# Second graph layer's row gathers: up to four underway in the loop instead of three

## What is computed

```
h = (x @ W.T).reshape(n, 8, 64)
src, dst = edge_index
e = leaky_relu(einsum(h[src], a_src) + einsum(h[dst], a_dst), 0.2)
e = e * (1 + et_emb[edge_type]) * edge_weight[:, None]
e = exp(e - max over the edges of each dst)
alpha = e / (sum over the edges of each dst + 1e-10)
out[dst] += h[src] * alpha            # the messages
out = layernorm(out + x) * gamma + beta
```

## Time and profile before

| what | value |
|---|---|
| median of three runs | 1776.36 us |
| the profiled execution, own time | 1784.84 us |
| span of the profiled execution | 1783.1 us |
| PE busy in the span | 1662.2 us, 93% |
| DVE, ACT, POOL busy | 883.9, 500.9, 652.3 us |
| first and last gather of the layer start at | 1080.67 and 1259.09 us |

### The profile page before, as it was taken

One profiled execution on the slowest core, in us unless ns is written; L12 is line 12 of the kernel. 1 busy time (PEld: TensorE's weight loads), 2 busy tenths in 40 slices (PEclk: granted clock), 3 DMA queues, 4 the chain that ended last, 5 costly groups with the idle time before them and its releaser, 6 DMA issues.

```text
span 1783.1 us, 23533 instructions
## 1 busy us (share of the span) xinstructions
PE 1662.2 (93%) x7303; PEld 940.2 (53%) x7304; DVE 883.9 (50%) x2161; ACT 500.9 (28%) x1586; POOL 652.3 (37%) x756
## 2 busy tenths in 40 slices
PE   6989999999899999999999998797899999999998
PEld 4534444446655546455556766432444555555655
DVE  8878888888834443443443157785623101111322
ACT  1134444447422414133231225110200111111234
POOL 5868787873232323324342613666200000000000
PEclk9999999999999999999998997899899999999999
DMA  8031101005423123232216734356326121310020
GB/s 315 1 104 25 60 25 60 25 8 132 141 58 128 54 90 83 58 110 55 74 49 153 276 96 146 111 162 174 100 72 217 50 91 53 100 59 24 5 68 18
DMA packets 119614, 161.76 MB, mean 91 GB/s; under 512 B 49497, under 2 KB 61721, under 8 KB 119154
## 3 DMA queue, kind: packets, MB, share of 16 engines
q1 hardware_dynamic: 93056, 115.43, 21.0%
q0 software_dynamic: 18592, 29.91, 6.3%
q10 hardware_dynamic: 7890, 15.44, 2.7%
HBM read 145.26 MB, written 15.47 MB: 90 GB/s over the span
## 4 chain that ended last, share of the span: by engine, by line
PE 81%; DVE 9%; DMA 5%; issue 2%; ACT 2%; POOL 1%; ACTq 0%; DVEq 0%; POOLq 0%; SPq 0%
PE psum L373 79%; DMA ring<-tab_h,sd_t 2%; DMA arena<-tab_h,sd_t 1%; DVE stats L470 1%; DVE ring L1299 1%; DVE xn L2067 0%; PE psum L1028 0%; DVE xn L2073 0%; POOL ring L630 0%; DVE xn L2086 0%; ACT xT L414 0%; PE psum L2302 0%; DMA x<-in_x 0%; DVE ring L666 0%; DMA tab_h<-arena 0%
## 5 line engine op out<-in xcount | busy, mean ns | idle before, releaser
L373 PE MATMUL psum<-arena 128*128 128x384 f32 (+9 forms) x1804 | 315.3, 331 | 21.1 <-DVE arena L2688 8.0
L373 PE MATMUL psum<-arena,ring 128*128 (+1 forms) x1504 | 326.0, 363 | 9.5 <-issue 6.2
L373 PE MATMUL psum<-xT,ring 128*128 128x384 f32 x928 | 310.7, 495 | 6.8 <-ACT xT L414 4.2
L373 PE MATMUL psum<-ring,arena 128*128 128x512 f32 (+1 forms) x570 | 262.8, 604 | 15.3 <-DVE ring L666 10.5
L373 PEld LDWEIGHTS psum<-arena 128*128 128x128 f32 (+5 forms) x1804 | 195.1, 154 | 148.8 <-issue 74.7
L373 PE MATMUL psum<-ring,xT 128*128 128x512 f32 x552 | 251.1, 608 | 1.1 <-issue 0.7
L373 PEld LDWEIGHTS psum<-xT,ring 128*128 128x128 f32 x928 | 178.2, 193 | 133.2 <-issue 17.6
L373 PEld LDWEIGHTS psum<-arena,ring 128*128 128x128 bf16 (+1 forms) x1504 | 139.4, 115 | 131.3 <-issue 29.9
L373 PEld LDWEIGHTS psum<-ring,arena 128*128 128x128 f32 (+1 forms) x570 | 99.2, 187 | 140.4 <-issue 139.3
L1079 ACT ACTIVATE ring<-ring 128x128 f32<-128x128 f32 x416 | 123.3, 297 | 173.4 <-DVE ring L1365 161.4
L373 PEld LDWEIGHTS psum<-ring,xT 128*128 128x128 f32 x552 | 104.8, 195 | 124.1 <-issue 121.7
(11 more groups left out here) (478 smaller groups left out, 1737.0 us busy)
## 6 DMA issues: line engine op xcount, KB each, us to landing
ring<-in_L_ffn_w SPq DMA_DIRECT2D x22, 1024.0 KB, 7.3
ring<-in_L_gnn_m_w SPq DMA_DIRECT2D x8, 1024.0 KB, 6.1
ring<-in_L_ffn_expert_weights SPq DMA_DIRECT2D x8, 1024.0 KB, 5.5
ring<-tab_key ACTq DMA_DIRECT2D x24, 256.0 KB
ring<-in_L_gnn_Wv SPq DMA_DIRECT2D x5, 1024.0 KB, 5.0
tab_w<-xn SPq DMA_DIRECT2D x6, 768.0 KB, 15.3
ring<-in_L_gnn_Ww SPq DMA_DIRECT2D x4, 1024.0 KB, 18.6
ring<-in_L_gnn_wq SPq DMA_DIRECT2D x4, 1024.0 KB, 5.3
```

The source lines that it names most:

```text
L373: return nc.tensor.matmul(o, a, b, start=start, stop=stop)
```

## The change

The limit in the loop goes from three to four. The 39 gathers ahead of the loop keep theirs of two. No instruction is added, removed or moved on any engine; in the 59 gathers from T = 39 on, the wait ahead of a gather is on the tile four places earlier instead of three.

```diff
-        UNDERWAY = (2, 3)
+        UNDERWAY = (2, 4)
```

## The result

The changed kernel takes 1769.26 us, the median of 8 runs (1761.73 to 1774.70), against 1776.80 us, the median of 8 runs of the kernel before (1774.51 to 1782.00). The ratio is 0.995 with a 95% interval of 0.9932 to 0.9968. The prediction was 8.1 us less; the medians differ by 7.5.

The account below looks back on a forecast made before the run. The supply of row tiles, spaced by the limit of three gathers underway, was taken as the bound; 58 steps at 1.40 us, 81.2 against 89.34, give 8.1 us less, from 1776.36 to 1768.3 us, range 1764 to 1777.5.

Parts of the forecast that it names:

- The bound and the place: In this layer's gather loop, the gathers' spacing, 1.54 us a tile from T = 39 to T = 97, sets the end.
- PE's two halves: PE's row tiles: 56 back to back at 0.99 us each, then 42 at 1.52 us, paced by the supply of tiles.
- The limit of three is what POOL waits for: Loop gathers wait on a 4.35 us cycle shared by three tiles, 1.45 us each; four would make it 1.09.
- Spacing with four: POOL's gathers T = 39 to T = 97: 1.40 us a tile, 58 steps in 81.2 us against 89.34.
- one bad meeting in seven: Loop gathers on POOL: six tiles at 1.25 us and one long at 2.09, together 9.6 us for seven.
- 0.2 for a slower landing: In the loop with four underway, 0.2 us more per seven tiles allowed for slower landings, giving 9.8 us.
- Does depth slow the landing?: Loop landings: bounded between no growth and 1.52 us more in the cycle, which would leave the spacing unchanged.
- The 0.77 us per step: Cycle growth from two underway ahead of the loop (3.58 us) to three in it (4.35); another would give 1.28 a tile.
- The meetings with DVE: Free-running loop gathers may meet DVE's instructions anywhere; bad meetings seen cost 0.85, 0.52 and 5.62 us.
- the slower rival: Loop gathers run into DVE's multiplies, over half caught, 0.40 us lost on average: 6.4 us more, 1782.8 us; chance 0.18.
- Nothing behind the loop gives it back: Work behind the layer hangs on its end and moves by the same amount, so the full 8.1 us reaches the kernel.

Follow-up runs that it names:

- the control: Kernel before with three underway in the loop, profiled again, one far load's count asserted at run time: 1778.21 us, ratio 1.0002.
- experiment 3: Kernel before with two underway in the loop instead of three: 1812.44 us, ratio 1.0199.
- Experiment 4: Kernel before with DVE's multiply cut to 8 of 512 columns: 1772.65 us with three underway in the loop, 1792.97 us with four.
- The thin multiply: DVE's multiply cut to 8 of 512 columns, here with four underway in the loop, against the kernel before: 1792.97 us, ratio 1.0089.
- four everywhere: Kernel before with four underway both ahead of the loop and in it: 1801.13 us, ratio 1.0123.

## Why the prediction was right

**The bound and the place.** The chain, PE's two halves and the spacing of the gathers were read rightly; the 58 steps returned in the control as 89.33 us, and changing the depth alone moved them to 124.31, 82.4 and 81.6 us.

**The limit of three is what POOL waits for.** Right. With four the idle time beyond 0.30 us over the 58 steps fell from 9.4 to 0.9 us.

**Spacing with four.** Forecast 1.40, measured 1.42 in both profiles (82.34 and 82.46 us). T = 51 to T = 93 took 60.77 and 60.19 us, where about 59 had been named, and single landings took up to 5.65 us, where under 4.5 had been named. The forecast had 0.945 + 0.30 and one bad meeting in seven, 9.6 us for seven, plus 0.2 for a slower landing. The real sum is: 58 x 1.245 = 72.2, plus 0.9 still waited, plus 9.1 by which the gathers ran longer than 0.945 us. I had about 7 in that last place (58 / 7 x 0.84) and 1.7 for the landing. The two errors nearly cancelled, which is luck.

**Does depth slow the landing?** The 0.77 us per step was a wrong reading. It compared two underway ahead of the loop with three inside it, and experiment 3 shows that the place made more than half of the difference: two in the loop have a cycle of 4.29 us, not 3.58, and from there to three it is 0.2 to 0.3, and to four about 0.1 by the median landing. What makes the cycle shorter ahead of the loop was not isolated. There POOL waits for one semaphore ahead of a gather and in the loop for two.

**The meetings with DVE.** The worry was right in kind and too dear in price: they cost 9.1 us with four and 7.7 with three, so freeing the gathers added 1.4 us. Experiment 4 shows that they are DVE's multiply, since they shrink to 2.5 us without it. The rule of the Trainium skill ("SBUF — State Buffer", "Who interferes with whom") on two SBUF inputs agrees with that in kind; some gathers still ran beside a multiply at 0.95 us, as T = 52 did. That a gather falls in step with the multiplies, as the slower rival needed for 0.40 us each, did not happen: 9.1 / 59 is 0.15.

**Nothing behind the loop gives it back.** By the medians, right: 7.5 and 9.0 us less in the two sets of runs, against 7.0 in the steps. The rest, up to 2 us, is within the spread of the runs.

**What the prediction missed** is a rival that ends on the slower side by another way: PE and DVE held up, with nothing in the program to wait for, when POOL issues without a pause. It stayed away in the changed kernel, where the longest row of gathers less than 1.32 us apart is five (six in its second profile), as DVE's one-hot instruction and its multiplies lengthen one here and there. The thin multiply took that away (28 in a row) and cost 24 us. The prediction had nothing that would have shown how near this was, so that it stayed away is luck too. It came in no profile whose rows were all shorter than that, but rows of eight passed without it in four profiles, and what in the chip the gathers take from the other engines was not tried.

## What to carry to other kernels

Where an engine issues transfers under a limit of so many underway, divide the cycle (issue to landing, plus the delay behind the wait) by the limit and compare it with the engine's own time per transfer: deeper helps until the second is the larger, and then stops at once. Look at each stage with its own limit, not only at the one whose wait is visible: ahead of the loop, where nobody seemed to wait for rows, one more underway was worth three times what the loop gave. And treat the pauses of a queue as something that other engines may live on: test one step deeper in each place apart. When it gets slower, look for an engine that starts long after everything that it waits for is done: the name beside its idle time ("issue", "remote", or the engine behind it) does not say so by itself.

## What the runs showed of the hardware

- With gathers of 256 KB issued each 1.25 us without a pause, PE, with nothing to wait for, did one matmul each 0.70, 1.40 or 2.80 us, for up to 24 us, and DVE began one instruction at least 24 us and another at least 9 us after all that it waits for. It was seen behind unbroken rows of 6 to 28 gathers, in two kernels. Rows of eight passed without it in the loops of four others, so the length of the row does not decide alone. Neither does the mean spacing (1.39 us in the loop of four everywhere, with a stop, and 1.39 with eight underway, without), nor the rate of bytes (183 GB/s in one such stretch and 197 in one of the eight underway without it). The profiles also record transfers of instructions beside the gathers. In four everywhere there is none from 1120 to 1152 us, and one right behind, as PE comes back. Which is cause and which effect was not tried.
- A gather's landing, start to DVE's begin, took 3.7 to 3.8 us (medians) whether three, four, five or eight could be underway, and 3.36 with two.
- POOL starts its next gather 0.72 us (median) after DVE's begin on the tile that both wait for, with a full or with a thin multiply on DVE.
- One gather in some profiles lasts 5.6 or 8.2 us instead of 1 (T = 32 in the first profile, T = 31 in the second one with four underway), both beside back-to-back DVE work. It was seen in 2 of 14 profiles. The scattering was 5.9 and 7.6 us longer there than in the next profile of the same kernel.
